# Building a sparse adjacency matrix: one compare-and-weight on a joint key in place of two one-hots and their product

## What is computed

```python
# layer 0: five hops with the same attention shares a
for _ in range(HOP):
    msg = f[src] * a[:, :, None]
    agg = jax.ops.segment_sum(msg, dst, num_segments=n)
    f = (1.0 - ALPHA) * agg + ALPHA * feat0
...
# layer 1: three convolutions, norm = dinv[src] * w * dinv[dst], with loops of weight 1
h = x @ W
msg = h[src_a] * norm[:, None]
out = jax.ops.segment_sum(msg, dst_a, num_segments=n) + b
```

## Time and profile before

| what | value |
|---|---|
| median of 3 runs | 6661.69 us |
| profiled execution, first to last instruction | 7657.2 us |
| scoring of the edges (806 gathers) | about 171 to 1570 us |
| hop 0 and what is before it | about 1570 to 2088 us |
| hops 1 to 4, with the build | 2088 to 7084 us |
| second layer's convolutions | 7084 to 7657 us |
| busy: tensor engine, VectorE, GpSimd | 4337.6, 3899.7, 4067.5 us |

### The profile page before, as it was taken

The page is one execution under the profiler, slowest core; times in us unless marked ns, Lnnn a source line. Parts: engine busy times, 40 slices in busy tenths (PEclk is TensorE's granted clock), DMA queues, the critical chain, the costliest instruction groups (busy, mean ns, idle before and its releaser), DMA issues.

```text
span 7657.2 us, 92403 instructions
## 1 busy us (share of the span) xinstructions
PE 4337.6 (57%) x19868; PEld 3742.3 (49%) x19869; DVE 3899.7 (51%) x8771; ACT 419.7 (5%) x1409; POOL 4067.5 (53%) x4073
## 2 busy tenths in 40 slices
PE   3544434426767777755555544555553555554799
PEld 1433434415567666744444433444443444443699
DVE  7655545578745555435555534555543555553411
ACT  0111101110000000000000000000000000000100
POOL 1566656611066666656666665666665666666000
PEclk9555555558955555555555555555555555555899
DMA  2334454415522222212222212222222222222476
GB/s 65 97 117 124 117 128 124 123 29 147 165 62 64 64 63 63 60 53 65 64 65 65 65 50 64 65 64 65 65 61 54 65 64 65 64 64 50 153 269 238
DMA packets 538438, 671.65 MB, mean 88 GB/s; under 512 B 102388, under 2 KB 423419, under 8 KB 528412
## 3 DMA queue, kind: packets, MB, share of 16 engines
q0 software_dynamic: 143008, 320.73, 15.7%
q1 hardware_dynamic: 391970, 345.94, 14.6%
q10 hardware_dynamic: 3418, 4.48, 0.2%
HBM read 511.17 MB, written 160.80 MB: 88 GB/s over the span
## 4 chain that ended last, share of the span: by engine, by line
PE 24%; another core or an unknown queue 23%; issue 22%; DVE 21%; DMA 4%; DVEq 3%; POOL 1%; ACT 1%; SPq 1%; ACTq 0%; POOLq 0%; PEldq 0%; PEld 0%
PE ps L889 6%; PE ps L901 6%; PE ps L1114 6%; DVE gap L1193 4%; DVE U L1218 4%; DVE U L1158 3%; PE ps L1002 2%; DMA U<-edge_fe 2%; DVE gap L1177 2%; POOL U L695 1%; DVEq L1177 1%; PE ps L995 1%; DVE gap L1181 1%; DVEq L1193 1%
## 5 line engine op out<-in xcount | busy, mean ns | idle before, releaser
L695 POOL DMA_INDIRECT U<-tab_f,stage x3224 | 3191.1, 990 | 2077.8 <-issue 951.7
L901 PE MATMUL ps<-U 128*125 128x128 f32 x8160 | 2131.9, 418 | 460.4 <-DVE U L1218 231.1
L901 PEld LDWEIGHTS ps<-U 128*125 128x125 f32 x8160 | 1731.7, 301 | 675.0 <-issue 674.9
L889 PE MATMUL ps<-gap 128*128 128x125 f32 x2816 | 842.1, 453 | 1708.2 <-issue 1168.8
L889 PEld LDWEIGHTS ps<-gap 128*128 128x128 f32 x2816 | 657.3, 324 | 1893.6 <-issue 1299.4
L1193 DVE SCALAR_TENSOR_TENSOR gap<-gap,U,ps 128x125 f32<-128x125 f32 x1408 | 487.9, 347 | 1820.8 <-remote 1397.5
L695 POOL DMA_INDIRECT U<-tab_he,stage x806 | 834.1, 1035 | 657.1 <-ACT stage L758 313.6
L1158 DVE TENSOR_TENSOR U<-dloc,iota_p 128x500 f32<-128x500 f32 x1225 | 834.2, 681 | 580.2 <-DMA U<-tab_f,stage 517.7
L1002 PE MATMUL ps<-U 125*128 x1632 | 421.5, 440 | 645.4 <-ACT U L795 438.7
L1218 DVE TENSOR_TENSOR U<-U,ex_it 128x512 f32<-128x512 f32 x1020 | 709.1, 695 | 0.0
L1002 PEld LDWEIGHTS ps<-U 125*128 125x128 f32 x1632 | 362.5, 327 | 705.1 <-issue 705.1
(11 more groups left out here) (235 smaller groups left out, 2414.2 us busy)
## 6 DMA issues: line engine op xcount, KB each, us to landing
adj<-gap SPq DMA_DIRECT2D x1408, 64.0 KB
edge_fe<-U SPq DMA_DIRECT2D x204, 256.0 KB
U<-edge_fe SPq DMA_DIRECT2D x204, 256.0 KB, 3.0
U<-tab_f,stage POOLq DMA_INDIRECT x3224
ex_it<-adj SPq DMA_DIRECT2D x30, 1600.0 KB, 6.2
U<-adj SPq DMA_DIRECT2D x30, 1600.0 KB, 6.2
fe_a<-adj SPq DMA_DIRECT2D x15, 1600.0 KB, 6.2
U<-tab_he,stage POOLq DMA_INDIRECT x806
```

The lines of the kernel that those rows point to most:

```text
L695: pool.indirect_dma_start(to[:, k, j, :], None, table, bass.IndirectOffsetOnAxis(ap=stage[:, k, j:j + 1], axis=0)).then_inc(got[k], 16)
L889: mm = nc.tensor.matmul(ps[:, 7 * BANK + j * CELL:7 * BANK + (j + 1) * CELL], hot_p[:, k % 2, j, :], prod[:, k % 2, j, :], start=True, sto ...
L901: mm = nc.tensor.matmul(ps[0:BN, bass.ds(b * F, F)], hot[:, k, j, :], ga[:, k, j, :], start=False, stop=False, skip_group_check=True)
```

## The change

The columns are prepared once, after hop 0: the weight is set to zero where the target lies outside the window (two instructions), and `win_b` becomes the joint key 5 x bucket + target within the window (one instruction). In each build step the right factor of an item is then one instruction over 125 columns, which compares the counter 0 to 124 with the item's key and multiplies by its weight. The bucket's one-hot, the two small one-hots, the product, their tiles and the wait on `build_link` are gone.

```diff
@@ tiles and semaphores
-        hot_bk = gap_part(2, BG, NB)
-        hot_d = gap_part(2, BG, WN)
-        build_link = sem("build_link")
@@ build_factors
-                v.tensor_tensor(hot_bk[:, k % 2], win_b[:, bass.ds(i, BG)].unsqueeze(2).to_broadcast([P, BG, NB]),
-                                iota_bn[:, 0:NB].unsqueeze(1).to_broadcast([P, BG, NB]),
-                                ALU.is_equal).then_inc(build_link, 1)
                 for j in range(BG):
-                    v.tensor_scalar(hot_d[:, k % 2, j, :], iota_bn[:, 0:WN], win_dd[:, bass.ds(win_item(s, r, k, j), 1)],
-                                    win_w[:, bass.ds(win_item(s, r, k, j), 1)], ALU.is_equal,
-                                    ALU.mult).then_inc(build_link, 1)
-                dve.wait_ge(build_link, r * (SLOTS * (BG + 1)) + (steps_before(s) + k + 1) * (BG + 1))
-                v.tensor_tensor(prod[:, k % 2].rearrange("p j (b d) -> p j b d", d=WN),
-                                hot_bk[:, k % 2].unsqueeze(3).to_broadcast([P, BG, NB, WN]),
-                                hot_d[:, k % 2].unsqueeze(2).to_broadcast([P, BG, NB, WN]),
-                                ALU.mult).then_inc(prod_ready, 1)
+                    i = win_item(s, r, k, j)
+                    ins = v.tensor_scalar(prod[:, k % 2, j, :], iota_bn, win_b[:, bass.ds(i, 1)], win_w[:, bass.ds(i, 1)],
+                                          ALU.is_equal, ALU.mult)
+                ins.then_inc(prod_ready, 1)
@@ after hop 0
                     dve.wait_ge(targets_ready, 1)
                     dve.wait_ge(cols_in, 16)
+                    link(v.scalar_tensor_tensor(out=win_w[:], in0=win_dd, scalar=0.0, in1=win_w[:], op0=ALU.is_ge,
+                                                op1=ALU.mult))
+                    link(v.scalar_tensor_tensor(out=win_w[:], in0=win_dd, scalar=float(WN - 1), in1=win_w[:],
+                                                op0=ALU.is_le, op1=ALU.mult))
+                    link(v.scalar_tensor_tensor(out=win_b, in0=win_b, scalar=float(WN), in1=win_dd, op0=ALU.mult,
+                                                op1=ALU.add))
```

More of the change, by code:

```diff
@@ L76 @@
 CELL = NB * WN
+assert CELL == BN
 ROW = P
```

## The result

| | before | after |
|---|---|---|
| median of 20 runs each | 6663.11 us | 6652.48 us |
| profiled execution | 7657.2 us | 6651.7 us |
| VectorE busy in the program | 3899.7 us | 3605.2 us |
| 3224 gathers of the hops, mean | 990 ns | 966 ns |

The ratio is 0.998, with a 95% interval from 0.9974 to 0.9987: faster, by 10.6 us from one median to the other, between 9 and 17 us by the interval. The forecast was 32 us. The direction and the range held, the size did not: it is a third of what was forecast.

A forecast was written before the change was run, and what follows sets the result against it. The prediction took GpSimd's chain of gathers as the bound: 48 us back from the product, less 11 us for the new instructions and 5 us for the masks, 32 us faster, 6629.7 us; range 6540 to 6690 us.

The forecast's parts named there:

- GpSimd is the bound in the runs; a hop takes 1065 us: Hops 1 to 4: GpSimd goes from gather to gather, 1065 us per hop, 4260 us for four instead of 4996.
- the inference from 1069.5 against 995.5 us: GpSimd's 1069.5 us of index waits mostly belong to the profiled execution, which was 995.5 us longer than the runs.
- 253 us of VectorE's time saved, none of it on the path: Build steps: VectorE saves 0.36 us in each of 704, all beside GpSimd's 5.16 us per step.
- The new instruction holds up gathers for 11 us: Build steps: the 1408 new compare-and-weight instructions delay GpSimd's gathers by 11 us in all.
- Rival 2: Build steps: the new pair holds the descriptor writer, up to 141 us, 6760 us; 6689 at half the steps; chance 0.17.
- The masks cost 5 us: Seam of hops 0 and 1: three new preparing instructions stand unhidden ahead of the additions, 5 us once.
- Removing the product gives back 48 us: Build steps: 353 of 3224 gathers were held by the product; without it GpSimd regains 48 us.
- Rival 1: Gathers freed from the product run into the one-hots or multiplication instead, leaving 6655 to 6667 us; chance 0.21.
- the mean gather of 979 ns: Sign in the changed kernel's profile: the hops' gathers average near 979 ns instead of 990.

The follow-up runs named there:

- before_again: The unchanged kernel before, run once more for a second profile; profiled span 6709.7 us, of which 4240 us for the four hops.
- early_pause: onehots_early with a dead reduction of 250 columns directly ahead of the one-hots; 6644.1 us, ratio to before 0.9909.
- onehots_early: The changed kernel with the message one-hots of hops 1 to 4 moved ahead of the wait for the gathers; 6837.5 us, ratio to before 1.0201.
- after_again: The changed kernel unaltered, run once more on the chip of most experiments; 6699.7 us, ratio to before 0.9997.
- pause_behind: The changed kernel with a dead reduction of 250 columns directly behind the multiplication in each build step; 6701.7 us, ratio to before 1.0001.

## Why the prediction was right or wrong

- *GpSimd is the bound in the runs; a hop takes 1065 us.* Right in size: 1060 in before_again, with 15 us to the first gather and 10 to drain it, and the inference from 1069.5 against 995.5 us held. But GpSimd doesn't set the pace alone: the step closes over the landing and VectorE's multiplication, 5.14 us where four free gathers take 4.98.
- *253 us of VectorE's time saved, none of it on the path.* Right that it lies beside the path; the idle time grew by 316 us on chips of one speed. The new instruction took 341 ns in the median for my 336, the fast form, but two of them take 0.51 us from start to start of what follows (3009.67 to 3010.18 above) and not 0.60.
- *The new instruction holds up gathers for 11 us.* It was 0.1 us, 2 gathers. Rival 2 is out for this place. VectorE's instruction is the one that waits: up to 581 ns. The Trainium skill's page SBUF — State Buffer, section "Who interferes with whom", would have had it lock out the descriptor writer. For instructions with two SBUF inputs the trace agrees (the multiplication held 515 to 762 of 3224 gathers, table above). For this one it depends on the place: in after, 3 of them began 0.12 to 0.21 us ahead of a gather's start, in early_pause 330 did and held 286 gathers for 0.05 us each, and in onehots_early, with the one-hots close behind, it had a part in 231 us. The rival had part of the mechanism, for another order of VectorE.
- *The masks cost 5 us.* Right: 4.98 us from the first of them to the additions.
- *Removing the product gives back 48 us.* This is the step that failed, twice. The term was read from an execution in which VectorE was thrown out of its rhythm and ran four steps in a burst; there the product met 353 gathers. In an even execution it met 175, once in a round of four steps, and held them for 25 us. And it was treated as additive: of the 25 us, 4 came back from the gathers on the experiments' chips, and by the clock of the first comparison some 10.6 + 5 = 16 (an estimate: what was measured, and what the preparing instructions took). A gather held by the product leads to one that the multiplication holds less. Rows of before_again show one such case; the counterpart is the step of after_again above:

```profile
3040.20 0.42 DVE L1181 TENSOR_TENSOR gap<-gap 128x250 f32<-128x250 f32 x1
3041.76 0.70 DVE L1158 TENSOR_TENSOR U<-dloc,iota_p 128x500 f32<-128x500 f32 x1 [1.14 <-DMA U<-tab_f,stage]
3042.38 0.68 DVE L1218 TENSOR_TENSOR U<-U,ex_it 128x512 f32<-128x512 f32 x1
...
3040.32 1.12 POOL L695 DMA_INDIRECT U<-tab_f,stage  x1 [0.30 <-issue]
3041.75 0.95 POOL L695 DMA_INDIRECT U<-tab_f,stage  x1 [0.30 <-issue]
3043.00 0.95 POOL L695 DMA_INDIRECT U<-tab_f,stage  x1 [0.31 <-issue]
3044.26 0.95 POOL L695 DMA_INDIRECT U<-tab_f,stage  x1 [0.30 <-issue]
```

The gather at 3040.32 loses 0.17 us to the product. Two gathers on, at 3043.00, the multiplication (until 3043.06) is nearly over and holds nothing back. The fourth starts at 3044.26, 2.50 us after the landing, where 2.40 is the pin: of 0.17 us lost, 0.10 reach the step. Rival 1 described this exchange, and its time, 6655 to 6667, was nearer than the forecast's; I gave it 0.21 because I looked for chance phases where there is a loop. It is luck that the mean gather of 979 ns, which the forecast named as a sign, was measured in after_again: before had 980 there, not 990, and the change took 1 ns off it where the forecast had 11.

Why the first chip gave 10.6 us and the others about none is argued, not shown. In the profile of after the fourth gather lands 2.67 us after its start in the median, on the others 2.74. The third gather would then begin 1.13 us after the landing by itself, next to the 1.155 at which it is let in, so that less of the product's delay could be swallowed. The same 0.06 us x 816 = 49 us is near what lies between the two times of the changed kernel, 6652 and 6700, and above the 37 between those of before, 6663 and 6700. No profile of before on such a chip, free of the long waits, was had.

## What to carry to other kernels

Time taken from an engine that isn't the bound comes back only through what it releases, so look for the loop that closes a step (here landing, multiplication, third gather, fourth gather, landing) and ask of each delay whether that loop already waits there. Where the bound is GpSimd's gathers, the place of VectorE's instructions relative to a gather's start, and what stands directly ahead of what, count for more than their length: the same dead reduction cost 208 us in one place of the changed kernel and nothing in another, and in a third it took 193 us off the kernel with the early one-hots. Before a rule is made of a coincidence, look for the same coincidence without the cost: 604 one-hots in the trace of after spoke against a rule that the next experiments were built on. And check the profiled execution against the runs before a term is read from it: counts of coincidences are the first thing that an uneven execution distorts.

## What the runs showed of the hardware

- A gather that begins while a VectorE instruction with two inputs in SBUF runs ends 0.82 us after that instruction's end, if that is later than its own 0.94 us (762 gathers by the multiplication in after_again). One that such an instruction follows out of idle time isn't held (604 one-hots begun 0.04 to 0.15 us behind a gather's start in after, at most 9 ns). The instructions with an input in PSUM (lines 1193 and 1163) held none.
- A compare-and-weight (one tile of columns as input and two scalars for each partition, 0.34 us) that begins 0.12 to 0.21 us ahead of a gather's start holds it until 0.82 us after its end: 286 of 330 in early_pause, 0.05 us each. Where an instruction with two inputs in SBUF follows it without a gap, the gather waits for that one too, though it began after the gather: 366 gathers in onehots_early, 0.63 us each.
- The compare-and-weight of 125 columns took 341 ns when free. Begun 0.41 to 0.54 us behind a gather's start it took up to 581 in after, and in pause_behind, where 522 begin some 0.43 us behind one, 567 ns in the median: there it waits for the gather.
- The landing time of the same gathers differs between chips by 0.06 us, 2.67 against 2.74, and the kernels, whose loop closes over it, by 0.5 to 0.7% in time. That the one makes the other is argued, not shown.
